# Scales of the feed-forward weights: from a sum of squares on ScalarE to a largest magnitude on VectorE, and the low halves cut on GpSimd

## The reference

```
xn = layernorm(x)
attn: h = rmsnorm(xn) * qkv_norm_w
      q, k, v = h @ ternary(qkv_w).T               # 16 heads of 32
      per chunk of 128 tokens and head:
        o = (q k^T * decay mask) v + (q * lam_t) S  # S: 32x32 state, carried on
        S = lam_T * S + (k * lam_rev)^T v
      out = rmsnorm(rmsnorm(o) ...) @ ternary(proj_w).T
ffn:  (silu(xn @ w_gate.T) * (xn @ w_up.T)) @ w_down.T   # hidden size 2048
x + attn + ffn
ternary(w): s = 1 / mean|w| ; clip(round(w * s), -1, 1) / s
```

## Time and profile before

| | before |
|---|---|
| median of 3 runs | 1431.05 us (1430.49 to 1431.59) |
| profiled execution: time, span | 1431.59 us, 1429.9 us |
| PE busy | 1366.5 us (96%) |
| PEld busy | 736.9 us (52%) |
| DVE busy | 931.6 us (65%), 1899 instructions |
| ACT busy | 479.0 us (34%), 877 instructions |
| POOL busy | 64.2 us (4%), 95 instructions |

### The profile page before, as it was taken

The page is one execution under the profiler, slowest core; times in us unless marked ns, Lnnn a source line. Parts: engine busy times, 40 slices in busy tenths (PEclk is TensorE's granted clock), DMA queues, the critical chain, the costliest instruction groups (busy, mean ns, idle before and its releaser), DMA issues.

```text
span 1429.9 us, 24260 instructions
## 1 busy us (share of the span) xinstructions
PE 1366.5 (96%) x8924; PEld 736.9 (52%) x8924; DVE 931.6 (65%) x1899; ACT 479.0 (34%) x877; POOL 64.2 (4%) x95
## 2 busy tenths in 40 slices
PE   4798789999999999999999999999999999999999
PEld 2354444555545554555545555455555555455554
DVE  6687776556665567656675567655666557755667
ACT  7755532323322323323223233232232332322322
POOL 5110000000000000000000000000000000000000
PEclk9999999999999999999999999999999999999999
DMA  7132224211251112611153112511126111361115
GB/s 287 59 126 82 82 47 91 77 31 45 60 134 30 30 45 60 147 32 36 32 103 97 32 43 56 127 54 30 45 59 134 32 28 45 75 132 31 44 31 118
DMA packets 200193, 101.95 MB, mean 71 GB/s; under 512 B 135584, under 2 KB 184736, under 8 KB 198432
## 3 DMA queue, kind: packets, MB, share of 16 engines
q1 hardware_dynamic: 199808, 100.45, 27.9%
q10 hardware_dynamic: 288, 0.01, 0.0%
HBM read 35.40 MB, written 8.39 MB: 31 GB/s over the span
## 4 chain that ended last, share of the span: by engine, by line
PE 83%; DVE 8%; ACT 3%; issue 2%; SPq 1%; DMA 1%; POOL 0%; ACTq 0%; DVEq 0%
PE bank L445 81%; PE bank L487 2%; DVE wg_lo L1183 1%; SPq L827 1%; DMA k_stack<-k_parts 1%; DVE xin L785 1%; DVE stage L647 1%; DVE sm L685 1%; ACT wg_lo L1033 1%; DVE wu_lo L1183 0%; DVE kl L695 0%; DVE sg L800 0%; DVE wd_lo L1183 0%; DVE arena L646 0%; DVE sm_lo L646 0%
## 5 line engine op out<-in xcount | busy, mean ns | idle before, releaser
L445 PE MATMUL bank<-wd_hi,arena 128*128 128x512 f16 x1024 | 318.7, 380 | 1.2 <-DVE wd_lo L1183 1.2
L445 PE MATMUL bank<-xt,wg_hi 128*128 128x512 f16 x1024 | 307.9, 382 | 5.2 <-issue 5.0
L445 PE MATMUL bank<-xt,wu_hi 128*128 128x512 f16 x1024 | 304.8, 379 | 5.3 <-DVE sg L800 4.7
L445 PE MATMUL bank<-xt,wg_lo 128*128 128x512 f16 x512 | 196.0, 383 | 0.0
L445 PE MATMUL bank<-wd_lo,arena 128*128 128x512 f16 x512 | 194.8, 380 | 0.0
L445 PE MATMUL bank<-xt,wu_lo 128*128 128x512 f16 x512 | 194.0, 379 | 0.0
L800 DVE SCALAR_TENSOR_TENSOR sg<-bank,small,sg 128x512 f32<-128x512 f32 x128 | 95.8, 749 | 130.5 <-PE bank L445 130.3
L634 ACT ACTIVATE arena<-sg 128x512 f16<-128x512 f32 x128 | 80.6, 629 | 296.5 <-DVE sg L800 296.5
L753 DVE SCALAR_TENSOR_TENSOR arena<-bank,small,arena 128x512 f32<-128x512 f32 x160 | 119.7, 748 | 85.1 <-PE bank L445 84.8
L445 PEld LDWEIGHTS bank<-wd_hi,arena 128*128 128x128 f16 x1024 | 100.5, 98 | 118.8 <-issue 2.8
L445 PEld LDWEIGHTS bank<-xt,wu_hi 128*128 128x128 f16 x1024 | 98.4, 98 | 114.4 <-issue 4.6
(11 more groups left out here) (186 smaller groups left out, 1613.8 us busy)
## 6 DMA issues: line engine op xcount, KB each, us to landing
q_stack<-q_parts SPq DMA_DIRECT2D x192, 64.0 KB, 2.2
k_stack<-k_parts SPq DMA_DIRECT2D x192, 64.0 KB, 2.2
xin<-x SPq DMA_DIRECT2D x34, 256.0 KB, 4.5
arena<-x SPq DMA_DIRECT2D x8, 1024.0 KB, 5.6
out<-arena SPq DMA_DIRECT2D x32, 256.0 KB, 3.4
stage<-gate_t SPq DMA_DIRECT2D x4, 1024.0 KB, 5.0
stage<-up_t SPq DMA_DIRECT2D x4, 1024.0 KB, 6.0
stage<-down_t SPq DMA_DIRECT2D x4, 1024.0 KB, 5.1
```

Of the source, the lines that this page charges most:

```text
L445: last = e.matmul(dst, a, b, start=start and n == 0, stop=stop and n == len(lhs) - 1)
```

## The change

Only block 0 is touched. For the 12 pieces of feed-forward weights, the magnitude is found by VectorE: four reductions of 128x512 to the largest magnitude, one quarter each (`WA n i`), and one over the four results. TensorE transposes the 128 row results (as a 128x128 broadcast) in place of the one-column sum, and VectorE takes the maximum of 128 values from PSUM before it makes the power of two (`power`, three instructions). The constants of the scales change with it.

For pieces 2 to 11 (`DVE_PIECES = 2`) the low part is a plain subtraction on GpSimd; for that ScalarE writes the scaled piece back over the raw one, a second copy in each `WH`. Pieces 0 and 1 keep the old form. GpSimd now also writes the ternary values of parts 2 to 4 itself, and ScalarE's `UM 2`, `UM 3`, `UM 4` go. `WH` of piece 4 waits for the ternary parts 2 and 3, since it writes over their raw buffer. `DVE_KINDS` has `WA` in place of `WC`, and the list of block 0 is written anew: four `WA` quarters in a row early on, and from piece 6 one quarter per item, so that a piece takes twelve places of the list in place of ten.

```
-    hidden = lambda n: [("WH", n, 0)] + [it for i in range(3) for it in (("WH", n, i + 1), ("WC", n, i))] + [("WC", n, 3)]
+    quarters = lambda kind, n: [(kind, n, i) for i in range(4)]
+    hidden = lambda n: [(kind, n, i) for i in range(4) for kind in ("WH", "WC")]
...
-        later += [("WA", n)] * (n > 5) + [rest, rest, ("WT", n), rest, ("WH", n, 0), rest, *hidden(n)[1:], ("WL", n + 2)]
+        later += [*quarters("WA", n) * (n > 5), rest, rest, ("WT", n), rest, *hidden(n), ("WL", n + 2)]
...
+DVE_PIECES = 2
...
     def cut(n, quarters=4):
-        return s_wlo, 4 * n + quarters
+        if n < DVE_PIECES:
+            return s_wlo["dve"], 4 * n + quarters
+        return s_wlo["pool"], 4 * (n - DVE_PIECES) + quarters
...
 GpSimd
-                    e.tensor_scalar(w, w, MAGIC + 1.0, MAGIC - 1.0, ALU.min, ALU.max).then_inc(s_clip_pool, 1)
+                    link(e.tensor_scalar(w, w, MAGIC + 1.0, MAGIC - 1.0, ALU.min, ALU.max))
+                    e.tensor_scalar(raw(n)[1], w, MAGIC, 1.0, ALU.subtract, ALU.mult).then_inc(s_tern_pool, 1)
+                elif kind == "WC" and n >= DVE_PIECES:
+                    i = it[2]
+                    e.wait_ge(s_whi, 4 * n + i + 1)
+                    hi_part, lo_part = piece_parts(n, i)
+                    e.tensor_tensor(lo_part, piece_raw(n, i), hi_part, ALU.subtract).then_inc(cut(n)[0], 1)
...
 ScalarE
-                    e.activation(piece_parts(n, i)[0], piece_raw(n, i), ACT.Copy, scale=ws[:, n:n + 1]).then_inc(s_whi, 1)
-                elif kind == "WA":
-                    e.wait_ge(ld_piece[n % 2], 16 * (n // 2 + 1))
-                    e.activation(squares_to(n), slot(n), ACT.Square, accum_out=pm[:, n:n + 1]).then_inc(s_red, 1)
+                    if PIECES[n] == ("down", 0):
+                        e.wait_ge(s_tern_pool, KT - POOL_TERNARY)
+                    last = e.activation(piece_parts(n, i)[0], piece_raw(n, i), ACT.Copy, scale=ws[:, n:n + 1])
+                    if n >= DVE_PIECES:
+                        last = e.activation(piece_raw(n, i), piece_raw(n, i), ACT.Copy, scale=ws[:, n:n + 1])
+                    last.then_inc(s_whi, 1)
...
 TensorE
-                        e.matmul(bank[:, 0:1], pm[:, n:n + 1].to_broadcast([P, P]), one[:, :], start=True, stop=True)\
-                            .then_inc(s_spread, 1)
+                        e.transpose(bank[:, 0:P], pm[:, n:n + 1].to_broadcast([P, P]), ident[:, :]).then_inc(s_spread, 1)
...
 VectorE
+                elif kind == "WA":
+                    i = it[2]
+                    e.wait_ge(ld_piece[n % 2], 16 * (n // 2 + 1))
+                    if n and i == 0:
+                        e.wait_ge(s_red, n)
+                    last = e.tensor_reduce(pm4[:, i:i + 1], slot(n)[:, i, :], axis=AX.X, op=ALU.max,
+                                           apply_absolute_value=True)
+                    if i == 3:
+                        link(last)
+                        e.tensor_reduce(pm[:, n:n + 1], pm4[:, :], axis=AX.X, op=ALU.max).then_inc(s_red, 1)
...
-                    e.tensor_scalar(am[:, n:n + 1], bank_of(it, 0)[:, 0:1], LEAST, None, ALU.max).then_inc(s_allmax, 1)
+                    e.tensor_reduce(am[:, n:n + 1], bank_of(it, 0)[:, 0:P], axis=AX.X, op=ALU.max).then_inc(s_allmax, 1)
...
-                elif kind == "WC":
+                elif kind == "WC" and n < DVE_PIECES:
```

More of the change, by code:

```diff
@@ L43 @@
 STEPS = 2 * GROUPS
-SMALL = 281
+SMALL = 280
 LN_EPS, RMS_EPS, OUT_EPS = 1e-5, float(np.finfo(np.float32).eps), 1e-6
 MAGIC = 1.5 * 2.0 ** 23
-LEAST = 1e-24
+LEAST = 1e-12
 X_SCALE = 2.0 ** 10
@@ L301, in build @@
     idle = table(1)
-    one = table(1)
     mv = table(2, 2)
@@ L374, in piece_parts @@
         return [w[:, :, P * h:P * (h + 1)] for w in (wg if kind == "gate" else wu)]
-    def squares_to(n):
-        kind, q = PIECES[n]
-        if kind == "down" and n < len(PIECES) - 2:
-            kind, q = PIECES[n + 1]
-        if kind == "down":
-            return wd[1][:, HPQ * q:HPQ * (q + 1), :]
-        return (wg if kind == "gate" else wu)[1][:, :, BLK * q:BLK * (q + 1)]
     def piece_raw(n, i):
@@ L462, in tensor_item @@
             if (kind, s) == ("Q", 0) and isinstance(blk, int):
-                e.wait_ge(s_tern, KT)
+                e.wait_ge(s_tern, POOL_TERNARY)
+                e.wait_ge(s_tern_pool, KT - POOL_TERNARY)
             if isinstance(blk, int):
@@ L926, in link @@
                 e.wait_ge(s_pool, done[0])
-            e.memset(one[:, :], 1.0).then_inc(s_ident, 1)
             e.memset(ident[:, :], 0.0).then_inc(s_ident, 1)
-            e.wait_ge(s_ident, 2)
+            e.wait_ge(s_ident, 1)
             e.affine_select(out=ident[:, :], in_=ident[:, :], compare_op=ALU.not_equal, fill=1.0, base=0,
```

44 lines of the change are left out of this document (22 added, 22 removed), and 2 rows, old and new, of the table at.

## The result

The changed kernel takes 1450.46 us (median of 4 runs, 1450.01 to 1451.58) against 1431.16 us for the kernel before, run beside it: ratio 1.0137, 95% interval 1.0119 to 1.0154. It is slower by 19.3 us, where +4.4 was forecast; the direction was right and the size, and with it the range, was not. The profiled execution took 1452.19 us, its span is 1450.1 us.

A forecast was written before the change was run, and what follows sets the result against it. No engine is full in block 0; the order in VectorE's and ScalarE's queues makes TensorE wait. Terms -1.2 + 3.0 + 0 + 1.0 + 1.6 = +4.4 us on 1431.05 gave 1435.5 us, range 1433.5 to 1440.

The forecast's parts named there:

- From 38 to 69 us: Block 0, pieces 2 and 3: TensorE's waits at `U 3` and `U 4` go, ScalarE is late next; -1.2 of 4.7 us.
- The port between VectorE and GpSimd: Block 0, first stretch: five two-input or large-copy VectorE instructions wait for GpSimd's; +3.0 us, bounds 0 and +6.
- half an instruction, 0.6: Average wait of such a VectorE instruction for GpSimd: each 0 to 1.5 us, taken as 0.6.
- Piece 4: 0: Last quarter of piece 4: ScalarE ready near 84.3 us, GpSimd at 86.1, against TensorE's old wait at 86.62; 0.
- The attention steps: Block 0, 88 to 205 us: changed items around K's stack +1.0 us, port waits in 8 steps +1.6.
- as full as before: VectorE in the attention steps: loses 32 cuts, gets 28 reductions and seven small ones, so its load stays.
- The transposition is one more small matmul: 0: `WT` of the twelve pieces: one more small matmul and 0.1 us each for the maximum, between other work; 0.
- the gains can't exceed the waits that are there: Attention steps: reason given for the bounds -3 and +4 on the items' sum of +1.0 us.
- (c): Much slower: GpSimd becomes the queue that ends last, its subtractions taking 1.4 to 1.9 us; +8 to +13, 1441 us; chance 0.11.
- (a): Faster: the 4.7 us at `U 3` and `U 4` are kept, GpSimd's instructions fall between VectorE's; 1427 us; chance 0.18.
- (b): No change: ScalarE's and VectorE's loads nearly cancel, K's stack chain sets block 0's pace; 1431.5 us; chance 0.23.
- signs of being right: Included blocks 1 to 7 at 169.0 us, subtractions near 1.2, silu 5 near 68.4, K's stack waits 2 to 3.5.

The follow-up runs named there:

- e7: The changed kernel with GpSimd's third ternary instruction as multiply by 1 and add -MAGIC, in place of subtract and multiply: 1443.68 us.
- C: The part of the change in which GpSimd writes the ternary values of parts 2 to 4; alone on the kernel before: 1442.19 us.
- e12: The kernel before with `U 2` read between the second and third cut of piece 2, `RD 0` and `RD 1` behind the reads: 1431.54 us.
- e10: The kernel before with its old list, but the magnitude reductions on VectorE in the place of each `WA`: 1445.51 us.
- e3: The changed kernel with all low parts back on VectorE and the ternary writes back on ScalarE: 1449.93 us.
- e9: The kernel before with the new list of block 0 and its rule for the low halves, squares still on ScalarE: 1443.53 us.
- e14: The changed kernel with the copies and cuts of piece 11 moved behind `K 7`: 1452.89 us.
- e15: The changed kernel with `WT` of pieces 5 to 11 one place later in the list: 1451.40 us.
- e6: The kernel before with twelve GpSimd instructions on dead buffers behind the last output, to time their forms by themselves; its time says nothing of the change.
- B alone: The kernel before with low parts of pieces 2 to 11 on GpSimd and ScalarE's second copy, old list: 1445.11 us.
- A: The part of the change with the magnitudes on VectorE and the new list; alone against the kernel before: 1449.93 us.
- e1: The changed kernel with `UM 2` to `UM 4` on ScalarE again, GpSimd only clipping in the ternary parts: 1442.96 us.

## Why the prediction was right in sign and wrong in size

| stretch | forecast | changed | e7, cheap pair |
|---|---|---|---|
| up to `D 0` | +1.8 | +8.5 | 0.0 |
| `D 0` to scores of step 4 | +0.7 | -2.4 | -1.3 |
| step 4 to step 7 | +1.9 | +13.8 | +13.9 |

The forecast column is the sum's terms by place: -1.2, +3.0 and 0; then the steps' items with 0.2 us of port each.

The sign was right in part by luck: the first stretch would be at 0.0 with the price that was assumed, and the steps, which lost, lost by other things than the ones that were summed.

**"From 38 to 69 us" held.** `U 3` starts at 45.85 with 1.35 us of wait (forecast: below 1), silu 4 at 56.9 (58.1). The walk has the read of `U 4` at 62.9 and silu 5 at 67.2, without the port; with the port's +3.0, which stands on this path, 65.9 and 70.2. They came at 66.33 and 71.83, and in e7, with the short instruction, at 64.97 and 69.13. So C's part in them is 1.4 and 2.7 us (besides the `HX`, one low half took 2.87 us beside the second long instruction). The wait of 4.42 at 58.84 hangs on the same `UL 3` as silu 4, late as the walk had it, since ScalarE copies piece 3 twice. e12 supports the reason given for keeping only 1.2 of 4.7 us, that ScalarE is late next. (Of the eight subtractions that left VectorE here, four had stood ahead of the read of `U 2`, four between it and that of `U 3`.)

**"The port between VectorE and GpSimd" failed in two prices.** Three ternary instructions "of 1.55" each: the third takes 5.55, and 7.41 in `RD 4`. The row used was of another pair of operations. From it follow the 2.7 us at silu 5 and 4.1 of the 4.61 at `D 0`, as `RD 4` took 11.4 us where 6.6 were priced; the other 1.7 of the 8.5 are slower matmuls and small waits between the two. The mechanism was right: VectorE's two-input instructions wait until GpSimd's is through. But "half an instruction, 0.6" for each was too little. In e7 `UL 3` takes 1.51 us, `HX 1` 1.94 and `HX 2` and `HX 3` 3.90, where 0.69, 0.74 and 1.41 stood before: 4.5 us over for four of them, where five were to give 3.0. With 4.5 the sum would have been +3.3 up to `D 0`. e7 is 0.7 late at silu 5 and 0.0 at `D 0`, so as much was absorbed on the way, and no run shows by what. That the total of this part comes close with the assumed price is thus in part luck too.

**"Piece 4: 0"** was right in e7 (0.50 us of wait against 1.23); in the changed kernel it is a wait of 4.61, for the third instruction of `RD 4`.

**"The attention steps" is the step that failed for most of the time.** In steps 1 to 3 it was rather too dark: -2.4 us came for +0.7, of which 1.5 is within what two traces of one code differ by, and K's stack gave 5.7 us of waits back. From step 4 to step 7 it gave +1.9 and 13.8 came. Three things were wrong in it.

First, "as full as before". Its count was off, to no effect: seven pieces go through the steps, not eight, so 28 cuts go and 24 reductions and 6 small ones come. But between step 4 and 7 VectorE's busy time went from 43.0 us to 51.4. There 11 cuts (8.1 us) made room for 12 reductions (8.0); the old list would have 8 (e10). The rest is in instructions that are the same. Their two inputs meet GpSimd's subtractions: six `SL` take 5.4 us where they took 4.1, two products of the attention output (L736, now L732) 2.4 for 1.4, and three pairs of state updates 5.1 for 2.2, one of the pair before and after:

```profile
L699 DVE SCALAR_TENSOR_TENSOR state<-state,small,kl 128x128 f32<-128x128 f32 x3 | 1.1, 351 | 0.1
```

```profile
L695 DVE SCALAR_TENSOR_TENSOR state<-state,small,kl 128x128 f32<-128x128 f32 x3 | 3.2, 1057 | 0.1
```

That is 5.2 us in these steps alone, where the sum had 0.2 a step. The small instructions of a third scale add 1.7, and the longer stretch takes in some of the next norm. Where the cuts stay on VectorE (e3) it is as full, 52.3 us, and the loss nearly the same, 12.5: the port took most of what the cuts had freed. And the new list moves work here: a piece takes twelve places for ten, so ScalarE makes 24 copies for pieces in that stretch (12 high parts, 12 second copies) where it made 9 and two squares. e9 prices the list at 8.6 us there without any reduction.

Second, the walk looked for who stands in front of K's stack. It did not ask who waits for what is new, and that is TensorE itself: its transposition in `WT` stands in the same queue as its products (4.23 us at piece 9, 2.07 at piece 11; all of `WT` in these steps 6.3 us, where the sum over ScalarE's squares had waited 0.7). "The transposition is one more small matmul: 0" left out its wait for VectorE. e14 and e15 add that this is not the fault of one place. `KV 6`, the one wait that was named, was named rightly, ScalarE's copies ahead of K's, and priced 1.4; it is 3.0 more than before (3.43 against 0.46).

Third, a wait costs more than its own length. Before and after, the same 32 matmuls of 128x512 take 379 and 458 ns, and of the 13.8 us 6.25 are such slower work; over the whole span it is 8.6 of 20.2 us, give or take 1 (in e6 the same code up to step 7 has 1.1 us more of busy time than in the kernel before). The stretch from 60 to 80 us is an example, before and then after:

```profile
60.00:80.00 20.00, 19.38 (x108) 10.91 (x107) 13.28 (x31) 16.84 (x25) 4.33 (x2) 1.00 0.11 43
```

```profile
60.00:80.00 20.00, 15.08 (x64) 6.83 (x62) 17.77 (x31) 8.92 (x14) 13.94 (x6) 0.85 0.00 0
```

After the waits of 4.42, 2.61 and 2.31 us around this stretch the clock is granted at 0.85, a part of it at the lower of its two levels, where without them it was 1.00. Behind the 4.61 us at `D 0` a whole stretch is granted half of the full clock, 0.50:

```profile
96.00:100.00 4.00, 4.00 (x11) 1.48 (x10) 1.30 (x3) 0.42 (x2) 0.00 (x0) 0.50 0.66 254
```

No term of the sum had this, and none of its bounds: "the gains can't exceed the waits that are there" bounds gains alone. The Trainium skill, page "TensorE: Matmul & The Clock Gate", section "Part 1: The HAM clock gate", has TensorE's clock halved after too little activity, and the trace agrees: 0.50 here, and 1.00 in the busy stretches of the loop.

**The rivals.** (c), much slower, had named GpSimd's subtraction as what grows. That took 1.16 us in the median, as forecast; single ones took up to 1.87, and the last two of piece 4, on which (c) hung, 1.43 each. What delayed them at `D 0` was the instruction ahead. (a) and (b) are out: "28.8 us go, 24.4 come" on ScalarE was nearly right as a sum (479.0 to 476.9 us busy) and said nothing, since ScalarE's length was not what counted. Of the signs of being right, the period of 169.0 us and the subtraction's price came; silu 5 within 2 us of 68.4 did not (71.83), nor waits of 2 to 3.5 us for K's stack in steps 1 and 2 (0.69 and 0.68).

What stays open: through which of its moves the list costs 8.6 us from step 4 to 7, and why B alone costs 8.4 us in block 0 but takes 7.3 back on top of A, most of it before step 4 (+0.4 in e3, -4.9 in e1). Moving single items changed only where TensorE waits.
